# One pool of eight PSUM banks and an order for each engine from a list schedule, in an attention and mixture-of-experts block

## The reference, cut to what matters

```python
q, k, v = (x @ Wq, x @ Wk, x @ Wv), 16 heads of 8, rope on q and k
attn = softmax(causal(q k^T / sqrt(8)));  x = layernorm(x + (attn @ v) @ Wo)
logits = x @ router_w.T + experts_bias;  top 2 of 8 experts, softmax over the two
g, u = x @ w1[e], x @ w3[e]  (256 wide);  eo = (silu(g) * u) @ w2[e]
x = layernorm(x + sum of the two experts' eo, weighted + the same form with sw1, sw3, sw2)
```

## Time and profile before

| what | value |
|---|---|
| median of 3 runs | 780.66 us (780.32 to 781.21) |
| the profiled execution's own time | 776.18 us |
| its span, first to last instruction | 774.1 us |
| busy: PE, DVE, ACT, POOL | 600.5, 475.7, 323.9, 322.0 us |
| mean granted clock of PE | 0.864 of full speed |
| bytes moved by DMA | 94.08 MB, mean 122 GB/s |

### The profile page before, as it was taken

One profiled execution on the slowest core, in us unless ns is written; L12 is line 12 of the kernel. 1 busy time (PEld: TensorE's weight loads), 2 busy tenths in 40 slices (PEclk: granted clock), 3 DMA queues, 4 the chain that ended last, 5 costly groups with the idle time before them and its releaser, 6 DMA issues.

```text
span 774.1 us, 14746 instructions
## 1 busy us (share of the span) xinstructions
PE 600.5 (78%) x4363; PEld 381.2 (49%) x4363; DVE 475.7 (61%) x1957; ACT 323.9 (42%) x771; POOL 322.0 (42%) x530
## 2 busy tenths in 40 slices
PE   3378988887878889888887998887898887786650
PEld 1123224424534565466544754655566665586640
DVE  3477747675537777776568877765578731644342
ACT  2016543563226455643364447524464455213320
POOL 4033431262275223424686326218447445442313
PEclk9567868978679999999899899979799999868985
DMA  3742220220224634622455345413575375435741
GB/s 92 214 143 87 63 91 2 76 83 8 70 89 141 185 93 130 180 93 86 153 163 149 94 151 157 127 47 122 159 217 169 93 210 165 133 102 158 203 111 54
DMA packets 80062, 94.08 MB, mean 122 GB/s; under 512 B 10224, under 2 KB 61168, under 8 KB 79984
## 3 DMA queue, kind: packets, MB, share of 16 engines
q1 hardware_dynamic: 75888, 84.75, 37.3%
q0 software_dynamic: 4096, 8.40, 3.4%
HBM read 70.37 MB, written 22.35 MB: 120 GB/s over the span
## 4 chain that ended last, share of the span: by engine, by line
PE 51%; issue 15%; DVE 15%; POOL 8%; ACT 6%; DMA 3%; SPq 1%; another core or an unknown queue 0%; POOLq 0%; ACTq 0%; DVEq 0%
PE ps L826 12%; PE ps L732 11%; PE ps L686 9%; PE ps L838 7%; PE ps L673 4%; POOL yg L506 3%; DVE sums L903 3%; ACT probs L548 3%; DVE gate L1029 2%; POOL rows_in L496 1%; PE ps L773 1%; DVE acc L1046 1%; PE ps L744 1%; POOL qk L332 1%; ACT th L607 1%
## 5 line engine op out<-in xcount | busy, mean ns | idle before, releaser
L903 DVE CUSTOM_DVE_ANT_0 sums<-ps,mask_sb 128x384 bf16<-128x384 f32 (+3 forms) x512 | 222.0, 486 | 51.9 <-PE ps L686 43.1
L484 POOL TENSOR_SCALAR_AFFINE_SELECT probs<-probs 128x256 f32<-128x256 f32 (+1 forms) x320 | 114.7, 364 | 263.7 <-ACT probs L548 260.6
L686 PE MATMUL ps<-stack 64*128 64x128 bf16 (+3 forms) x1024 | 160.2, 334 | 61.1 <-ACT probs L548 20.1
L548 ACT ACTIVATE probs<-ps 128x512 f32<-128x512 f32 x320 | 183.5, 597 | 44.2 <-PE ps L686 41.6
L1029 DVE SCALAR_TENSOR_TENSOR gate<-th,ps 128x256 f32<-128x256 f32 x131 | 54.8, 418 | 122.3 <-ACT th L607 104.2
L826 PE MATMUL ps<-xgT,w_tile 128*128 128x128 f32 x792 | 119.7, 299 | 12.0 <-issue 6.8
L686 PEld LDWEIGHTS ps<-stack 64*128 64x128 bf16 x1024 | 48.9, 97 | 144.0 <-DVE negmax L903 38.8
L826 PEld LDWEIGHTS ps<-xgT,w_tile 128*128 128x128 f32 x792 | 106.4, 209 | 21.9 <-issue 15.2
L607 ACT ACTIVATE th<-ps 128x256 f32<-128x256 f32 x131 | 50.3, 384 | 110.5 <-PE ps L826 89.6
L732 PE MATMUL ps<-probs,va 128*32 128x512 f32 (+3 forms) x1024 | 90.9, 503 | 6.8 <-POOL probs L484 2.8
L838 PE MATMUL ps<-w_tile,hid 128*128 128x128 f32 x396 | 70.6, 305 | 24.7 <-DVE hid L1037 13.1
(11 more groups left out here) (105 smaller groups left out, 605.0 us busy)
## 6 DMA issues: line engine op xcount, KB each, us to landing
w_tile<-in_experts SPq DMA_DIRECT2D x99, 384.0 KB
stack<-parts_scratch SPq DMA_DIRECT2D x112, 128.0 KB
rows_out<-y_routed SPq DMA_DIRECT2D x99, 64.0 KB
parts_scratch<-parts SPq DMA_DIRECT2D x16, 384.0 KB
xg<-rows_in SPq DMA_DIRECT2D x21, 256.0 KB
rows_in<-zeros SPq DMA_DIRECT2D x2, 1472.0 KB, 10.5
x_t<-in_x SPq DMA_DIRECT2D x8, 256.0 KB, 2.9
x_r<-in_x SPq DMA_DIRECT2D x8, 256.0 KB
```

The source lines that it names most:

```text
L484: pool.affine_select(out=area, in_=area, compare_op=ALU.is_ge, fill=0.0, base=0, pattern=pattern, channel_multiplier=-1).then_inc(masked, 1)
L548: act.activation(probs[:, (s * NB + v) % PRING, :], ps[:, SC + v % 2, :], ACT.Exp, scale=SCALE).then_inc(exp_done, 1)
L686: return pe.matmul(ps[:, bank, at:at + width], here[:, stationary, at_s:at_s + P], here[:, moving, at_m:at_m + width], start=True, stop=True)
L903: ins = dve.tensor_tensor_reduce(sums[:, use % 2, at:at + w], ps[:, M + use % 2, at:at + w], mask_sb[:, S - w:S], -1.0, 3.0e38, ALU.add, A ...
```

## The change

The common list is gone. At build time `plan()` runs through time with one clock per engine. Each piece of work has a priority (its old kind of place, from `AT` and `LATER`, both with new numbers), a list of what it needs (`needs`), and two durations from a table `COST`: how long the engine is taken and how long until the result is there. At each moment an engine takes, of the work that is ready, the one of the lowest priority number. For PE work must also find banks: all eight are one pool, a bank is free once its reader has finished in the plan, and scores and max units may hold at most four banks each (`HELD`). What comes out is the fixed order of each engine and a fixed bank for each use, with the number of that use on its bank (`bank_of`, `nth`). On the chip PE waits, before it writes, for the reader of the use before on that one bank (`take`). Each bank has a semaphore for full and one for free. `burst` is split into `score_pair` and `max_pair`, which the plan places each for itself. The computation, its instructions' shapes and the SBUF buffers are as before, and so are the sizes of the rings there.

```diff
-AT = dict(values=2.39, v=9.96, rows1=12.08, maxima1=11.92, heads_T0=3.87, heads_T1=5.09, out_T=6.97, out=8.09,
...
+AT = dict(values=3.1, v=9.39, rows1=1.85, maxima1=11.32, heads_T0=1.6, heads_T1=4.56, out_T=7.38, out=-16.83,
...
+COST = dict(
+    pe=dict(x_T=(480, 700), project=(1850, 2100), v=(950, 1200), max_rows=(120, 350), values=(2500, 2700), heads_T=(950, 1200),
+            out_T=(480, 700), out=(950, 1200), x1_T=(480, 700), router=(950, 1200), count=(600, 850), rank=(1800, 2050),
+            T=(120, 350), gate=(970, 1200), down=(490, 700), score_pair=(370, 620), max_pair=(370, 620)),
+    act=dict(x_T=(490, 650), rope=(920, 1100), rest=(920, 1100), v=(490, 650), values=(490, 650), out=(490, 650),
...
+SWITCH = 200
...
+HELD = dict(score_pair=4, max_pair=4)
...
+READ = dict(ln1_stats=650, router=450, count=300, rank=900)
...
-    for n in range(BLOCKS * B + LEAD):
-        for b in range(NU):
-            add(2 * (NU * (n - LEAD) + b), "burst", n, b)
+    for s in range(B):
+        for w in range(NB // 2):
+            add(NB * s + 2 * w, "score_pair", s, w)
+            add(NB * s + 2 * w - 2 * NU * LEAD, "max_pair", s, w)
...
+    def uses_of(kind, key):
...
+    def needs(engine, kind, *key):
...
+            if kind == "score_pair":
+                n = NB * s + 2 * key[1] + 1 - PRING
+                found = [("pe", "values", n // NB, n % NB // UPG)]
+                return found + [("sp", "maxima", s, key[1] // (2 * NU))] if key[1] % (2 * NU) == 0 else found
+            if kind == "max_pair":
+                half = key[1] // (2 * NU)
...
+    def plan():
...
+        ends, holder, held, tiled = {}, [None] * 8, [0] * 8, False
...
+        while tries:
+            tries.sort()
+            now, engine = tries.pop(0)
+            if now < free[engine]:
+                continue
+            best = None
...
+                if waits[part] or due[part] > now or best is not None and parts[best] <= parts[part]:
+                    continue
+                if engine == "pe":
+                    wanted = len(uses_of(kind, part[2:]))
+                    open_banks = [n for n in range(8) if holder[n] is None or read.get(holder[n][0], now + 1) <= now]
+                    if len(open_banks) < wanted:
+                        continue
+                    others = sum(1 for n in range(8) if n not in open_banks and holder[n][1] == kind)
+                    if others + wanted > HELD.get(kind, 8):
+                        continue
+                best = part
+            if best is None:
+                continue
+            kind, key = best[1], best[2:]
+            queue[engine][kind].pop()
+            lines[engine].append((kind, key))
+            taken, lasts = COST[engine][kind]
+            if engine == "pe":
+                if kind in ("score_pair", "max_pair"):
+                    taken, lasts, tiled = (taken, lasts, True) if tiled else (taken + SWITCH, lasts + SWITCH // 2, True)
+                else:
+                    tiled = False
+                for use, reader in uses_of(kind, key):
+                    n = min((n for n in range(8) if holder[n] is None or read.get(holder[n][0], now + 1) <= now),
+                            key=lambda n: read[holder[n][0]] if holder[n] else -8 + n)
+                    bank_of[use], nth[use] = n, held[n]
+                    holder[n] = (reader, kind)
+                    held[n] += 1
+            read[best] = now + READ.get(kind, lasts)
+            free[engine] = now + taken
+            ends[best] = now + lasts
+            left -= 1
+            tries.append((now + taken, engine))
+            if engine in ("dve", "act"):
+                tries.append((read[best], "pe"))
...
     def line(engine):
+        return lines[engine]
...
-    RING = ("x_T", "v", "values", "max_rows", "out_T", "out", "x1_T", "router", "count", "rank", "T", "down")
...
-        SC, M, GU, R = 0, 2, 4, 6
...
-        m_full = sem("m_full"); m_free = sem("m_free")
-        ring_full = [sem("ring_full0"), sem("ring_full1")]; ring_free = [sem("ring_free0"), sem("ring_free1")]
+        bank_full = [sem(f"bank_full{n}") for n in range(8)]; bank_free = [sem(f"bank_free{n}") for n in range(8)]
...
+            return ps[:, bank_of[use], :]
...
+            return full(*use), nth[use] + 1
...
+            def take(*use):
+
+                if nth[use] > 0:
+                    pe.wait_ge(free(*use), nth[use])
...
-            def ring_bank_free(*use):
-                if ring_use[use] >= 2:
-                    pe.wait_ge(free(*use), ring_use[use] // 2)
...
-            def burst(n, b):
-
-                scored = n - LEAD
-                if scored >= 0:
-                    s, block = scored // BLOCKS, scored % BLOCKS
-                    half = scored // 2
-                    first = NU * 2 * scored + 2 * b
-                    if scored % 2 == 0 and b == 0:
-                        pe.wait_ge(max_in, (half + 1) * 48)
-                    for pair in range(2):
-                        if first + pair >= 2:
-                            pe.wait_ge(exp_done, first + pair - 1)
-                        for at_piece, (k, j, at) in enumerate(PAIR_UNITS[b]):
-                            last = score(SC + pair, half, pair, 2 * (block % 2) + k, 1, j * P, 0, j * P, S - j * P, at)
-                        last.then_inc(st_ps, 1)
-                if n < BLOCKS * B:
-                    s, block = n // BLOCKS, n % BLOCKS
-                    half = n // 2
-                    if n % 2 == 0 and b == 0:
-                        pe.wait_ge(stacked[half % PLACES], STACK * (half // PLACES + 1))
-                    for pair in range(2):
-                        use = m_use[("max", s, 2 * NU * block + 2 * b + pair)]
-                        bank_free(use)
-                        for k, i, at in MAX_UNITS[b]:
-                            last = score(M + use % 2, half, pair, 2 * (block % 2) + k, 0, i * P, 1, 0, i * P + P, at)
-                        last.then_inc(m_full, 1)
+            def score_pair(s, w):
+
+                block, b = w // NU, w % NU
+                half = 2 * s + block // 2
+                if w % (2 * NU) == 0:
+                    pe.wait_ge(max_in, (half + 1) * 48)
+                for pair in range(2):
+                    take("scores", s, 2 * w + pair)
+                    for k, j, at in PAIR_UNITS[b]:
+                        last = score(bank("scores", s, 2 * w + pair), half, pair, 2 * (block % 2) + k, 1, j * P, 0, j * P,
+                                     S - j * P, at)
+                    last.then_inc(full("scores", s, 2 * w + pair), 1)
+
+            def max_pair(s, w):
+
+                block, b = w // NU, w % NU
+                half = 2 * s + block // 2
+                if w % (2 * NU) == 0:
+                    pe.wait_ge(stacked[half % PLACES], STACK * (half // PLACES + 1))
+                for pair in range(2):
+                    take("max", s, 2 * w + pair)
+                    for k, i, at in MAX_UNITS[b]:
+                        last = score(bank("max", s, 2 * w + pair), half, pair, 2 * (block % 2) + k, 0, i * P, 1, 0, i * P + P, at)
+                    last.then_inc(full("max", s, 2 * w + pair), 1)
 
             def max_rows(s, half):
-                pe.wait_ge(m_free, m_use[("max", s, half * NB // 2 + NB // 2 - 1)] + 1)
-                ring_bank_free("max_rows", s, half)
```

More of the change, by code:

```diff
@@ L173, in build_block @@
     step_of = {key: i for i, key in enumerate(STEP)}
+    READER = {"out_T": ("act", "out"), "out": ("dve", "ln1_stats"), "max_rows": ("dve", "max_rows"), "router": ("dve", "router"),
+              "count": ("dve", "count"), "rank": ("dve", "rank"), "gate": ("dve", "glu"), "project": ("dve", "project"),
+              "heads_T": ("dve", "heads_T"), "score_pair": ("act", "scores"), "max_pair": ("dve", "max")}
+    order_of = {}
+    for at, _, kind, key in sorted(events, key=lambda event: event[:2]):
+        order_of.setdefault(kind, []).append((at, key))
@@ new lines, in build_block @@
+    loads_in = {g: (TILES[g] + XQ - 1) // XQ for g in range(len(SORTED))}
+    def uses_of(kind, key):
+        engine, reader = READER.get(kind, ("act", kind))
+        if kind in ("score_pair", "max_pair"):
+            units = [(key[0], 2 * key[1] + pair) for pair in range(2)]
+            return [((reader, *unit), (engine, reader, *unit)) for unit in units]
+        if kind in ("project", "heads_T"):
+            return [((kind, *key, n), (engine, reader, *key)) for n in range(2)]
+        return [((kind, *key), (engine, reader, *key))]
@@ L183, in build_block @@
+    weight_use, rows_use, routed_use, shared_use, max_use = {}, {}, {}, {}, {}
     for kind, key in line("pe"):
[L184 to L191 removed]
@@ L192, in build_block @@
-        if kind == "heads_T":
-            for n in range(2):
-                m_use[(kind, *key, n)] = len(m_use)
         if kind == "T":
@@ L201, in build_block @@
             rows_use[key] = len(rows_use)
+    for kind, key in line("dve"):
```

(15 more changed lines are left out.)

420 lines of the change are left out of this document (304 added, 116 removed).

## The result

The change takes 686.31 us (median of 4 runs, 682.61 to 689.81) where the kernel before takes 780.93 beside it: ratio 0.878, 95% interval 0.873 to 0.884. That is 94.6 us off, where I had forecast 55, and 4 us outside my range at its fast end. The profiled execution ran 689.81 us with a span of 687.8, so 86.3 us came off the span of 774.1.

What follows compares the result with a forecast made beforehand. PE was taken as nearest its limit but not at it, losing to pauses and the lower clock. 4 + 30 + 16 + 15 - 10 = 55 us off 776.2 gave 721.2, at the median 726 us; range 690 to 775.

Steps and rivals of the forecast that it cites:

- (b): PE's waits for banks still being read, 40.3 us outside the start: three quarters go, 30 us; ends 0 and 40.
- (c): PE's data waits, expert steps and x1 transposes: 12 of 16.4 us and 4 of 12.8 go, together 16.
- (d): PE's work at the lower clock, 70 to 750 us, costs 59 us; fewer pauses bring back a quarter, 15.
- (a): The start, 29 to 70 us: sequence 1's projections fill the first-stack pause, sequence 2's take their place; 4 us off.
- (e): New waits where the chip runs late against the order and banks fixed at build time; 10 us charged.
- Waits for `probs`, `negmax` and `on` after 70 us below 15: Sign the forecast is right: PE's waits for these three readers of banks total below 15 us after 70 us.
- Granted clock above 0.88: Sign the forecast is right: PE's granted clock over the whole run stands above 0.88.
- `hid` below 6: Sign the forecast is right: the waits of `down` for `hid` in the expert steps fall below 6 us.
- PE's share above 80%: Sign the forecast is right: PE is busy above 80% of the span.
- PE near its limit: The pool keeps PE 90% busy from 70 to 676 us, 506 in place of 606: 677 us at the median; chance 0.12.
- The banks couple the engines: Each of PE's 1171 bank uses waits on a fixed bank, passing lateness between kinds: 21 us slower, 802; chance 0.17.
- The waits change only their names: Data behind bank waits come no sooner: 15 of the bank and data gains stay, 19 us off, 762; chance 0.13.

Runs made afterwards that it cites:

- Experiment 2: Kernel before with every engine's order unchanged, only the eight banks made one pool: 728.93 us, ratio 0.932; repeated 719.71 us, 0.938.
- Experiment 4: Kernel before, with PE made to wait for both banks of a pair ahead of its first unit: 809.20 us, ratio 1.036.
- Experiment 8: Old orders with pooled banks, x1's transposes and the steps behind them 1.5 units later: 738.11 us, ratio 0.962, against 0.932 and 0.938 without the edit.
- experiment 7: The change with the two zero fills of the row buffers issued behind a later stack load: 681.40 us, ratio 0.871; repeated 654.00 us, 0.851.
- experiment 6: The change with at most two banks each for score and maximum units: 710.22 us, repeated 681.58; separately, with six banks in place of eight: 714.26 us.
- 1 split banks: The change with its scheduler and numbers, but each kind confined to its two old banks: 785.47 us, ratio 1.002; repeated 757.69 us, 0.987.
- 3 old numbers: The change with AT and LATER of the kernel before, all else kept: 712.67 us, ratio 0.907; repeated 665.10 us, 0.870.
- 5 kept burst: The change with a maximum pair forced right behind its score pair: 708.32 us, ratio 0.907; repeated 668.16 us, 0.871.

## Why the prediction missed

**(b) Bank waits, the step that failed.** I took 30 of 40.3 us, and even my upper end was too low. The rows that I had added up did about what I said: the 45.6 us are 9.1 now, 4 of the difference lie in the head, and 4.8 came new (PE at the pairs for `ot`, 3.4, and `xgT`, 1.4), which leaves some 28. The mistake was to take them for the whole. "20.1 + 10.4 + ..." were the idle times of PE's matmul rows; by the weight loads' rows the pairs alone stood 76 us, and the part of this that lay under a running matmul I had put at nothing, as work. Experiment 2, the bank term by itself, gave 52 and 46 us (clock included). Experiment 4 shows where it had hidden: 24 to 32 us inside PE's busy time.

**(c) Data waits.** Near in sum, wrong in place. I expected 12 of 16.4 us of `hid` and 4 of 12.8 of x1. All of x1's went, and 5.0 of the 5.2 for xgT, while the router's for x1T rose by 2.4; `hid` fell from 9.5 to 3.1 us while attention runs (70 to 603 us before, 64 to 518 now) as the orders' spacing had said, but in the last stretch, where no pairs are left to put between, it rose from 2.8 to 13.6. Together 12.8 + 5.0 - 2.4 + 6.4 - 10.8 = 11 us for my 16. These rows move with the series: in the two quiet profiles of the change the router's wait for x1T is 0.2 to 0.4 us, but `hid` is 28 and 30 over the run, 8 and 9 of it while attention runs, so that little is left there of the gain from spacing. Experiment 8 warns of taking any such row as a price: removing 14.8 us of x1 from the other kernel cost 18.

**(d) The clock.** By the same working as in the prediction, the work at the lower level now is 0.12 x 76 + 0.18 x 319 + 0.04 x 63 + 0.32 x 54 = 86 us for 119, and half the difference, 16, came back; I took 15. A part of the 16 is not the clock but the hidden waits, which left the busy time that the working multiplies, so (b) and (d) overlap. From 70 to 198 us (now 64 to 151) the granted clock rose from 0.81 to 0.94, with PE's busy share from 82 to 88%; from 198 to 603 it stayed, 0.92 and 0.91, with 85 and 87%. By the Trainium skill (TensorE: Matmul & The Clock Gate, "What's actually happening") activity releases the throttled clock. The first stretch agrees; the second shows no gain. No run isolates the clock; this term is argued from rows.

**(a) The start.** 5.8 us for 4. The projections of sequence 2 did come in, and still PE's busy time fell by 12 us, 7.9 of them the pairs': the hidden waits again. The first stack did not slip (29.1 us). What came late was the maxima's rows, behind the zero fills; I had asked only whether the first stack would be late.

**(e) New waits.** 10 charged; the one found is that same wait, 8.1, worth 6 (experiment 7). What fixed orders lose to lateness elsewhere stays open; the series with the unexplained waits (last section) cost them more than the old orders.

**The signs I named.** Waits for `probs`, `negmax` and `on` after 70 us below 15: yes, 11. Granted clock above 0.88: 0.885. First pair near 29, 24 us at the end: 29.1 and 23.0. `hid` below 6: no, 20.8. PE's share above 80%: no, 79%, because half of the gain was busy time that fell.

**The rivals.** *PE near its limit* came closest in time, 677 us, partly by luck. It had 455 us of work at the higher clock from 70 to 676 us, busy 90% of 506. Now PE is busy 458 of 525 us, 87%, at a clock that did not come near 1.0 (0.91 in the long stretch); by the working of (d) that is some 423 us of work at the higher clock. Its work was too much by the hidden waits, and its clock too fast, and the two errors nearly cancel. *The banks couple the engines* is refuted by experiment 2, where mixing the banks alone takes off 46 us and more; experiment 6 points the same way. Its picture of the kernel before was also too clean: there ACT's `tanh` read the `gate` banks, and DVE read ring banks, so lateness passed between kinds already. *The waits change only their names* holds for `hid` and the parts' stack alone.

## What to carry to other kernels

Before pricing bank waits on PE, read the weight loads' rows beside the matmuls': where a pair is two units on the two halves of the array, a wait of the second for its bank lies under the first's run and counts as busy, and the gap between the two views is gain that a busy share hides. Buffers and order are to be judged together: here a pool was worth 46 us with the old order and a free order 8 without the pool, but 106 together. A wait that a shift takes away must be followed down its chain; a DMA that nobody waits for soon belongs behind the ones that somebody does.

## What the runs showed of the hardware

In the profiles of the first three series, of every kernel, ACT and DVE stand in waits that end with nothing shown in the trace (the profile names their releaser "remote", and "another core or an unknown queue" in the chain, though one core runs). Of the change, ACT's three largest, and one of them in the timeline:

```profile
ACT ot L858 <- remote: 22.6, 4, 7.0
ACT th L886 <- remote: 16.6, 8, 4.4
ACT y_routed L899 <- remote: 10.1, 8, 2.6
```

```profile
457.17 2.36 PE L1005 MATMUL ps<-probs,va 128*32 128x512 f32 x32
...
465.10 0.60 ACT L858 ACTIVATE ot<-ps 128x512 f32<-128x512 f32 x1 [6.98 <-remote]
...
465.75 0.60 PE L961 MATMUL ps<-stack 64*128 64x384 bf16 x2 [3.36 <-ACT ot L858]
```

`values` ends at 459.5, its copy starts 5.6 us later, and PE then waits for ACT. In the change and in its version with late zero fills (the run of 681.40 us), two programs nearly alike, they fall mostly on the same instructions: the copies of `values` wait 5.2, 7.0, 3.4 and 7.0 us in the one and 6.7, 7.0, 3.0 and 7.0 at the same four in the other, which has a fifth of 6.0. None of the quiet profiles has one; the kernel before has no quiet profile. It is not the chip alone: one chip ran the first series of experiments, with these waits, and the first quiet one. Before the change's third series (its 0.862) I had written down what should come if the kernel before ran near 768 us there: 0.857 to 0.865 and no such wait, and so it was. The sum of these waits in the first profile (both engines), and the medians of the two kinds of series:

```
kernel              sum of such waits   median with   quiet     less
before                     31.2            780.9      765.7     15.2
2 pool, old order          42.0            728.9      719.7      9.2
1 split banks              72.8            785.5      757.7     27.8
change                     87.5            686.3      659.7     26.6
6 two held                 88.5            710.2      681.6     28.6
7 late fills               91.4            681.4      654.0     27.4
3 old numbers             103.9            712.7      665.1     47.6
5 kept burst              117.7            708.3      668.2     40.2
```

The two grow together on the whole, the gain being 22 to 49% of the sum; that the waits are the cause is not shown, only that both are there or both are not. So part of a ratio here hangs on the series: the change stood at 0.878 in one and at 0.861, 0.862 in two others. What the engines wait for stays open; the trace has no row for it. The list-scheduled kernels differ more between the two kinds of series (27 to 48 us) than the two with the old orders (9 to 15).
